# Two mixture-of-experts layers in one kernel: the first layer's gate and up products in three rounded passes, weights rounded under the attention, and a new order of TensorE's work

## The reference

```python
# first mixture (H = 256); the second is the same with F = 512 and its own weights
logits = flat @ router_w.T                       # 4096 x 8
topk_vals, topk_idx = jax.lax.top_k(logits, 2)
topk_w = softmax(topk_vals)
g = einsum('sd,edh->esh', flat, w_gate)
u = einsum('sd,edh->esh', flat, w_up)
y = einsum('esh,ehd->esd', silu(g) * u, w_down)
out = einsum('esd,se->sd', y, dense_w)           # the two chosen experts, weighted
```

## Time and profile before

| | us |
|---|---|
| median of 3 runs | 954.91 (952.94 to 957.68) |
| the profiled execution | 959.59 |
| its span, first to last instruction | 957.9 |
| attention, about | 126 to 324 |
| first mixture's experts, about | 383 to 530 |
| second mixture's experts, about | 705 to 931 |

### The profile page before, as it was taken

One profiled execution on the slowest core, in us unless ns is written; L12 is line 12 of the kernel. 1 busy time (PEld: TensorE's weight loads), 2 busy tenths in 40 slices (PEclk: granted clock), 3 DMA queues, 4 the chain that ended last, 5 costly groups with the idle time before them and its releaser, 6 DMA issues. The chain is left out here.

```text
span 957.9 us, 18611 instructions
## 1 busy us (share of the span) xinstructions
PE 759.6 (79%) x4846; PEld 580.7 (61%) x4847; DVE 528.8 (55%) x1510; ACT 469.6 (49%) x1197; POOL 438.4 (46%) x492
## 2 busy tenths in 40 slices
PE   2896968888898756999999056569389999999980
PEld 1675846666665446566666035457358888888870
DVE  6787946777766459344443257764843333333326
ACT  2994435777775324444444156643234444334434
POOL 5000446776772000544443577720026666666744
PEclk9999887999998655999999657985569999999995
DMA  3000000000000140333332121104001111111117
GB/s 98 1 0 20 3 0 2 1 0 0 0 2 1 45 175 2 100 99 99 98 99 62 51 52 47 44 1 176 0 17 37 40 42 44 39 44 40 44 27 263
DMA packets 33165, 45.89 MB, mean 48 GB/s; under 512 B 8115, under 2 KB 22775, under 8 KB 32736
## 3 DMA queue, kind: packets, MB, share of 16 engines
q1 hardware_dynamic: 24256, 27.66, 8.9%
q0 software_dynamic: 8864, 17.72, 7.0%
HBM read 30.21 MB, written 15.60 MB: 48 GB/s over the span
## 5 line engine op out<-in xcount | busy, mean ns | idle before, releaser
L1833 POOL DMA_INDIRECT d_xg<-d_normed,d_gather x71 | 67.2, 946 | 123.6 <-PE ps L1889 66.8
L1094 DVE TENSOR_REDUCE negmax<-ps 128x2 f32<-128x512 f32 x128 | 82.4, 686 | 47.9 <-PE ps L930 47.9
L1833 POOL DMA_INDIRECT f_xg<-f_normed,f_gather x71 | 69.0, 971 | 83.2 <-PEq L1871 58.2
L1934 ACT ACTIVATE f_silu<-ps 128x512 f32<-128x512 f32 x71 | 42.4, 597 | 126.9 <-PE ps L1902 126.9
L1971 DVE TENSOR_TENSOR f_xgT_low<-ps,f_xgT 128x128 fp32r<-128x128 f32 x71 | 20.7, 292 | 144.9 <-ACT f_xgT L1938 144.9
L1839 POOL DMA_INDIRECT f_results<-f_y,f_scatter x71 | 71.9, 1013 | 61.9 <-DVE f_y L1965 53.3
L830 ACT ACTIVATE prob<-ps 128x512 f32<-128x512 f32 x128 | 69.6, 598 | 40.0 <-PE ps L949 40.0
L1896 PE MATMUL ps<-d_w_in,d_xgT 128*128 x142 | 79.5, 642 | 3.9 <-ACT d_xgT L1938 1.5
L1959 DVE TENSOR_TENSOR d_h<-ps,d_silu 128x256 f32<-128x256 f32 x71 | 30.1, 424 | 86.4 <-ACT d_silu L1934 86.4
L1917 PE MATMUL ps<-f_w_out,f_hT 128*128 x568 | 75.2, 275 | 0.6 <-DVE f_y L1965 0.6
L1917 PEld LDWEIGHTS ps<-f_w_out,f_hT 128*128 128x128 f32 x568 | 69.0, 192 | 0.8 <-issue 0.8
(11 more groups left out here) (369 smaller groups left out, 2053.7 us busy)
## 6 DMA issues: line engine op xcount, KB each, us to landing
d_results<-d_y SPq DMA_DIRECT2D x71, 64.0 KB
raw_weights<-in_f_in SPq DMA_DIRECT2D x16, 256.0 KB, 2.9
f_ys<-f_results SPq DMA_DIRECT2D x8, 512.0 KB, 6.4
X<-in_x SPq DMA_DIRECT2D x4, 512.0 KB, 5.8
d_normed<-X SPq DMA_DIRECT2D x8, 256.0 KB, 2.0
d_w_in<-in_d_in SPq DMA_DIRECT2D x1, 2048.0 KB, 7.8
f_normed<-X SPq DMA_DIRECT2D x8, 256.0 KB, 2.0
f_w_out<-in_f_out SPq DMA_DIRECT2D x1, 2048.0 KB, 9.3
```

What stands on the lines that cost most here:

```text
L1094: nc.vector.tensor_reduce(negmax[:, :, h // HG, col:col + 1], ps[:, 2 + h % 2, :].rearrange("p (t k) -> p t k", t=2), AX_X, ALU.max, negat ...
L1833: nc.gpsimd.indirect_dma_start(xg[:, n % 4, :], None, moe.xn_dram, bass.IndirectOffsetOnAxis(ap=moe.gather[:, n:n + 1], axis=0)).then_inc( ...
L1934: nc.scalar.activation(silu[:, at.b, :], GATE(at.b), ACT.Silu).then_inc(silu_ready, 1)
```

## The change

1. The first mixture's gate and up weights now come as two tensors, `d_w_high` and `d_w_low`, made during attention: SP loads the raw weights into `X` at the attention's start; in each of the 16 periods ACT rounds one piece of 128 x 256 into `high` after `keys`, and POOL subtracts it from the raw piece into `low` after `splits`.
2. `route` no longer loads `d_w_in`.
3. In `experts` of the first mixture, `gate_up` is three fp32r products of 512 columns instead of one fp32 product, and DVE gains `low_x`.
4. In both mixtures the order of PE becomes load_expert(s+1), transpose_x(s+1), gate_up(s), transpose_h(s-1), down(s-2), and ACT copies x before it does the gate.
5. PE's program of the first mixture is written out.
6. `y` has eight buffers instead of four in both mixtures.

```diff
-def written_out(stages, items):
+def written_out(stages, items, width=4):
...
+        @block.sync
+        def _(sp):
+            sp.dma_start(whole, next_dram.rearrange("p e f -> p (e f)")).then_inc(next_in, 16)
...
+                piece = bass.ds(n * PIECE, PIECE)
+                wait_apart(pool, next_high_ready, n + 1, passed_pool)
+                nc.gpsimd.tensor_tensor(whole_low[:, piece], whole[:, piece], whole_high[:, piece],
+                                        ALU.subtract).then_inc(next_low_ready, 1)
...
+                if known == 0:
+                    act.wait_ge(next_in, 16)
+                piece = bass.ds(n * PIECE, PIECE)
+                nc.scalar.activation(whole_high[:, piece], whole[:, piece], ACT.Copy).then_inc(next_high_ready, 1)
...
-            if not moe.split:
-                sp.dma_start(moe.w_in[:], w_in_dram).then_inc(moe.weights_in, 16)
...
-        y = sb("y", [P, 4, C])
+        y = sb("y", [P, 8, C])
...
-                if not moe.split:
-                    ins = nc.tensor.matmul(ps[:, 2 * at.b, 0:2 * F], xgT[:, at.b, :], of_expert(moe.w_in),
-                                           start=True, stop=True)
...
+                if 2 * F <= 512:
+                    outs = ((ps[:, 2 * at.b, 0:2 * F], slice(0, 2 * F)),)
+                passes = ((xgT, moe.w_high), (xgT, moe.w_low), (xgT_low, moe.w_high))
+                for i, (x, w) in enumerate(passes):
+                    for o, cols in outs:
+                        ins = nc.tensor.matmul(o, x[:, at.b, :], of_expert(w)[:, cols],
+                                               start=(i == 0), stop=(i == len(passes) - 1))
...
-            pipeline(pe, [(0, gate_up), (-1, load_expert), (-1, transpose_x), (1, transpose_h), (2, down)], SLOT_TILES)
+            stages = [(-1, load_expert), (-1, transpose_x), (0, gate_up), (1, transpose_h), (2, down)]
+            if split:
+                written_out(stages, SLOT_TILES)
+            else:
+                pipeline(pe, stages, SLOT_TILES)
...
-            stages = [(0, gate), (-1, copy_x), (1, copy_h)]
+            stages = [(-1, copy_x), (0, gate), (1, copy_h)]
...
+            dve.sem_inc(xg_ready, 1)
+            stages = [(-1, low_x), (0, hidden), (2, result)]
```

More of the change, by code:

```diff
@@ L713, in softmax_attention @@
                                       "out_ps", "bo_added", "tok_rd"))
+        whole, whole_high, whole_low = top.X[:], *(w[:].rearrange("p e f -> p (e f)") for w in halves)
+        PIECE = TOK // N
+        next_in, next_high_ready, next_low_ready = (k.sem(f"c_{s}") for s in ("next_in", "next_high", "next_low"))
         Q = ps[:, 4, :].rearrange("p (g t) -> p g t", g=2)
@@ L1180, with __init__ @@
     SLOT_TILES = (TOP * TOK + E * (P - 1)) // P
[L1182 removed]
+    def __init__(self, nc, k, hidden, tag, halves=None):
         self.F = hidden
         self.tag = tag
[L1187 to L1191 removed]
+        if halves is None:
+            halves = (k.sb(f"{tag}_{s}", [P, self.E, 2 * hidden], F32R) for s in ("w_high", "w_low"))
+        self.w_high, self.w_low = halves
         self.w_out = k.sb(f"{tag}_w_out", [P, self.E, hidden // P, C])
@@ L1497, in _, with route @@
             pipeline(dve, [(-4, moe_output), (2, normalise), (0, features), (1, sums), (3, statistics)], N, 4)
-def route(nc, top, moe, router_dram, w_in_dram, w_out_dram):
+def route(nc, top, moe, router_dram, w_out_dram):
     T, ps, ident = top.T, top.ps, top.ident
@@ L1848, in _ @@
                     scatter(step - 2)
-            for b in range(4):
-                pool.wait_ge(scattered[b], 16 * ((SLOT_TILES - b + 3) // 4))
+            for b in range(8):
+                pool.wait_ge(scattered[b], 16 * ((SLOT_TILES - b + 7) // 8))
         if moe.by_slot:
@@ L1926, in _ @@
         def _(act):
-            if not moe.split:
-                act.sem_inc(xg_ready, 1)
             act.sem_inc(hT_ready, 2)
@@ L1972, in low_x @@
                                         ALU.subtract).then_inc(xg_ready, 1)
-            low = []
-            if moe.split:
-                dve.sem_inc(xg_ready, 1)
-                low = [(-1, low_x)]
-            stages = low + [(0, hidden), (2, result)]
+            dve.sem_inc(xg_ready, 1)
+            stages = [(-1, low_x), (0, hidden), (2, result)]
             if split:
-                written_out(stages + [(0, split.low(dve))], SLOT_TILES)
+                written_out(stages + [(0, split.low(dve))], SLOT_TILES, 8)
             else:
-                pipeline(dve, stages, SLOT_TILES)
+                pipeline(dve, stages, SLOT_TILES, 8)
 def combine(nc, top, moe, out):
@@ L2151, in program @@
             with ExitStack() as first_layer:
-                first = Moe(nc, Kit(nc, first_layer), 256, "d")
-                route(nc, top, first, d["d_router"], d["d_in"], d["d_out"])
+                first = Moe(nc, Kit(nc, first_layer), 256, "d", halves)
+                route(nc, top, first, d["d_router"], d["d_out"])
                 with ExitStack() as side:
@@ L2156, in program @@
                 linear_attention(nc, top, d["lin_wq"], d["lin_wkv"], first)
-            route(nc, top, moe, d["f_router"], d["f_in"], d["f_out"])
+            route(nc, top, moe, d["f_router"], d["f_out"])
             experts(nc, top, moe)
```

47 lines of the change are left out of this document (20 added, 27 removed).

## The result

The changed kernel takes 914.57 us (median of 4 runs, 913.55 to 915.76); the kernel before, run beside it, takes 953.92 (950.24 to 957.68). The ratio is 0.9588, with a 95% interval of 0.9546 to 0.9629: 4.1% faster. The prediction said 918 and 904 to 934. The profiled execution took 913.55 us, its span is 911.8.

The account below looks back on a forecast made before the run. PE was taken to bound both expert stages. Savings of 28.0 us (first mixture) and 9.1 (second), less 0.3 for low_x, give -36.8: 922.8 from the profiled 959.59, 918 for the median; eight-in-ten range 904 to 934.

Parts of the forecast that it names:

- The tile of the first mixture: First mixture's experts: a tile falls from 1.97 to 1.57 us, saving 28.0 us over 70 tiles; bounds 19.6 and 34.3.
- The floor of 1.48: First mixture's tile if PE never waits: transposes 0.33, products 0.705, down 0.45, together 1.48 us.
- It saves 0.25 us a tile: First mixture's gate_up: three fp32r passes take 0.705 us against 0.96 for the one fp32 product.
- The hole and the late load: First mixture: PE's 0.12 us gap between down and gate_up, and 0.09 for a late weight load; the new order removes most.
- the loop: First mixture on PE: the loop's register instructions and branches cost 0.12 us a tile, 1.97 against 1.85 written out.
- Rival (b): First mixture: DVE or the sequencer takes the ring's place at 1.75 us a tile, saving 15.4 there; 930.7 us; chance 0.13.
- The second mixture: Second mixture's experts: only the order changes; 3.05 to 2.92 us a tile, saving 9.1 us; bounds 14.0 and a loss of 7.
- Rival (c): Second mixture gains nothing, as the expert's number is now loaded where nothing hides it: 927 us; chance 0.22.
- The margin of 0.7 us for gathers: Second mixture: a gather lands 4.6 us after the result, its transpose comes 5.3 us after it; fits by 0.7 us.
- Attention at nothing: Attention: 16 ACT copies (6.6 us) and 16 POOL subtractions (10 us in all) fit in idle time, cost 0.
- Rival (d): Attention: POOL's subtractions hold up DVE's rest of x, which PE waits for; 12.7 us lost, 931 us; chance 0.06.
- the starving of PE: First mixture: the written-out program starves PE of instructions, at most 20 us, 938 us; taken as nothing; chance 0.03.

Follow-up runs that it names:

- e9: Changed kernel, expert-number load behind gate_up, separate PSUM banks, covered waits dropped, second mixture's PE program written out: 963.72 us, ratio 0.9617 to the kernel before; first-mixture tile median 1.48.
- e4: Changed kernel with the load of the expert's number issued behind gate_up in both mixtures: 963.42 us, ratio 0.9603 to the kernel before; first-mixture tile 1.603 us.
- e5: Changed kernel with y's two PSUM buffers in two banks, so down waits for the result two tiles back: 966.22 us, ratio 0.9659 to the kernel before.
- e10: Changed kernel without three of PE's waits that earlier waits already cover: 969.88 us, ratio 0.9694 to the kernel before; first-mixture tile 1.618 us.
- e2: Changed kernel with the old order of stages on PE and ACT in both mixtures: 995.78 us, ratio 0.9909 to the kernel before; tiles 2.019 and 3.417 us.
- e6: Changed kernel with attention's added ACT copy and POOL subtraction each done twice per period: 975.27 us, ratio 0.9762 to the kernel before; attention's period 10.47 us.
- e3: Changed kernel with PE's program of the first mixture back in a hardware loop: 999.47 us, ratio 1.0138 to the kernel before; first-mixture tile 2.040 us.
- e1_fp32_product: Changed kernel with first mixture's gate_up as one fp32 product of rounded x and weights: 969.85 us, ratio 0.9698 to the kernel before; tile 1.680 us.

## Why the prediction was right, point by point

**The tile of the first mixture: right in size, wrong in its parts, and in that lucky.** 1.57 forecast, 1.585 measured; 28.0 us forecast and 70 x (1.971 - 1.585) = 27.0 us measured. The floor of 1.48 exists (e9's median). But the terms under it were mis-sized in ways that cancelled. "It saves 0.25 us a tile" for the passes is 0.07 when the other parts are there: it set 0.96, with a late load in it, against 0.705 without one, where the runs have 0.90 against 0.80. The hole and the late load, priced 0.12 and 0.09, and the loop, priced 0.12, are worth 0.29 together, close to their sum of 0.33, though neither the order nor the writing out gave its share alone. The loop's price was a difference between two stretches of the kernel before, where the order hid the load of the expert's number; in the new order the same loop costs 0.43.

**What lies on top of the floor.** The prediction put it between 1.48 and 1.69 by the sequencer's load and DVE's queue. Rival (b), the sequencer or DVE as the new bound, named the right place and the wrong size (1.75). The load alone is not it (e4), DVE's result alone is not (e5), the waits alone are not (e10); all together are, by the median and the number of periods at the floor (e9), not by the mean.

**The second mixture:** 2.92 forecast, 2.883 measured, 9.1 us forecast and 11.3 measured from the starts. Rival (c), no gain, is wrong on the first chip; on chip A e2 speaks for it, and on B and C the old order was not run. Its reason, the load of the expert's number, is not what holds the tile there: with the load behind gate_up (e4) it still takes 3.374 us. The margin of 0.7 us for gathers was really thin: PE waits for gathers even on the first chip (1.9 us), which the prediction had named as a sign that it is wrong. On the other chips it is not what sets the pace.

**Attention at nothing:** right, and even doubled (e6), though a subtraction on POOL takes 0.72 us and not 0.61. Rival (d) did not come: DVE's rest of x takes 416 ns mostly instead of 466, with the same longest one of 1259. In time none of the 16 overlaps with an added subtraction, so the run doesn't test the rule that the prediction named for it (GPSIMD Engine Reference, section Specifications, of the Trainium skill). Where the two engines do run beside each other for long, these traces agree with it: the one of 1259 ns lies beside POOL's operation on q and q_low for 0.98 us, in both kernels, and in e6 one of 909 ns beside POOL's subtraction of the mean for 0.63. Shorter overlaps, up to 0.34 us, go with 415 ns as well as with 490.

**Load, eight buffers, the starving of PE at nothing:** right. The 2 MB land in 7.7 us. One instruction queue carries 25 packets instead of 18, and 18 again in e3 with PE's loop, so the seven are PE's written-out program; its tiles on the first chip show no pause for them. That agrees with Runtime: NRT & Kernel Launch, section Instruction fetch mechanics, of the Trainium skill, by which such a fetch runs ahead and is mostly hidden.

**The sum.** -27.0 for the first experts, -11.3 for the second by the starts (-26.9 and -8.9 by the windows, which hold the ends too), nothing elsewhere: 36 to 38 us, against 36.8 forecast and 39.35 between the medians. The remaining 1 to 3.5 us are within what the two medians scatter. The profiled pair shows 46.1 because of the 6.3 us at the end of attention and in the route, where the granted clock differs, and 4.0 spread over the other stages.

## What to carry to other kernels

Price an edit beside the other edits, not beside the kernel as it is: a loop that costs 0.12 us a tile while a long product hides the sequencer costs 0.43 once the order has moved that cover away, and with the passes in place two edits that each left the tile at 2.0 us brought it to 1.61 together. Count PE's register instructions, waits and loads as a stream of its own, some 0.1 us each, and compare it with the floor of the matmuls. When single experiments all say "no change", several limits may lie together; take them away at once before you call the rest a property of the engine, and look at medians and counts beside the mean. When an engine starts late, look for the moment at which its semaphore was raised before you blame that engine.

## What the runs showed of the hardware

- PE's sequencer starts a wait or a register instruction every 0.10 to 0.14 us when nothing holds it, takes about 0.36 us of its stream for a register load, and 0.49 us for the three instructions of a loop's end, of which the branch is 0.21 (changed kernel and e3_loop).
- A product of 512 columns in fp32 hands over after 0.86 us when its weights are loaded in time (e1_fp32_product, one tile; 0.90 on average), three fp32r passes after 0.80 when the first load is late (changed kernel).
- The same program takes 914.6 us on one chip and 972.3 on chip B; the kernel before takes 953.9 and about 1,000 on A, B and C. In the second mixture a third of ACT's instructions (61 of 174) start over 1 us, up to some 3 us, after the end of the matmul that they wait for on chip B and none on the first; the semaphore increments by PE are recorded that much later, and ACT starts 0.02 us behind them.
